# A gated graph, attention and memory layer on one core: the edge matrix counted in two copies, and the row products one slot later

## What is computed

```python
edge_index = jnp.stack([src, dst])
xn = _layernorm(x, axis=-1)
x = x + gnn(xn, edge_index, edge_type) + mix(xn)       # two gated graph layers; two blocks of linear attention and an MLP
x = x + memory(_layernorm(x, axis=-1))

# one graph layer; w[r] is a sum over 30 bases of 512 x 512, weighted by att
x_j = x[col]
msgs = [sigmoid(x_j @ gate_w[r])[:, None] * x_j @ w[r] for r in range(2)]
msg = jnp.where((edge_type == 0)[:, None], msgs[0], msgs[1])
agg = jax.ops.segment_sum(msg, row, num_segments=1250)
return agg + x @ root + bias

# memory: 8 heads, each picks 8 of 65536 pairs of keys; 64 rows for each node
inner = jnp.einsum('bd,bhkd->bhk', x, w_down[indices])
vals = jax.nn.relu(inner) * jax.nn.softmax(scores, axis=-1)
out = jnp.einsum('bhk,bhkd->bd', vals, w_up[indices])
```

## Time and profile before

| what | value |
|---|---|
| median of 3 runs | 3177.79 us |
| lowest and highest run | 3175.93 and 3196.16 us |
| the profiled execution, its own time | 3188.18 us |
| its span, first to last instruction | 3186.4 us |
| busy: PE, DVE, ACT, POOL | 2657.5, 1516.1, 700.5, 1010.8 us |
| mean granted TensorE clock | 0.926 |

### The profile page before, as it was taken

The page is one execution under the profiler, slowest core; times in us unless marked ns, Lnnn a source line. Parts: engine busy times, 40 slices in busy tenths (PEclk is TensorE's granted clock), DMA queues, the critical chain, the costliest instruction groups (busy, mean ns, idle before and its releaser), DMA issues.

```text
span 3186.4 us, 28032 instructions
## 1 busy us (share of the span) xinstructions
PE 2657.5 (83%) x8756; PEld 1463.4 (46%) x8756; DVE 1516.1 (48%) x3729; ACT 700.5 (22%) x1527; POOL 1010.8 (32%) x823
## 2 busy tenths in 40 slices
PE   2897887998770299999899888789898998998887
PEld 1564555665330044444366455554544544454322
DVE  3556448999200000000122545157657656666675
ACT  0233222121210000110033422123232323322322
POOL 0003343444344200000000000026566556656676
PEclk9898998999895599999999989899999999999999
DMA  9601306676210123023300040038898898889998
GB/s 209 204 0 21 89 1 190 200 216 187 43 7 1 32 78 79 0 62 112 92 1 0 0 148 0 7 110 314 284 329 312 297 314 308 309 311 332 344 366 349
DMA packets 237785, 498.58 MB, mean 156 GB/s; under 512 B 98553, under 2 KB 98928, under 8 KB 233546
## 3 DMA queue, kind: packets, MB, share of 16 engines
q0 software_dynamic: 158720, 336.03, 31.5%
q1 hardware_dynamic: 76425, 156.38, 16.5%
q10 hardware_dynamic: 2550, 5.12, 0.4%
HBM read 476.77 MB, written 20.34 MB: 156 GB/s over the span
## 4 chain that ended last, share of the span: by engine, by line
PE 49%; DMA 26%; DVE 11%; issue 7%; POOL 3%; ACT 2%; another core or an unknown queue 1%; SPq 1%; POOLq 0%; DVEq 0%; ACTq 0%
DMA adj<-e_cnt,e_idx 21%; PE bank L1018 10%; PE bank L1243 10%; PE bank L1233 3%; PE bank L1223 3%; PE bank L1003 2%; PE bank L581 2%; PE bank L1180 2%; PE bank L562 2%; PE bank L550 2%; PE bank L557 2%; PE bank L1192 2%; DVE qv L1471 2%; DMA qv<-in_L_ffn_rows,qv 2%; PE bank L770 1%
## 5 line engine op out<-in xcount | busy, mean ns | idle before, releaser
L283 POOL DMA_INDIRECT adj<-e_cnt,e_idx x160 | 344.2, 2151 | 740.4 <-DMA adj<-e_cnt,e_idx 446.8
L1243 PE MATMUL bank<-qv,stage 125*125 125x512 f32 x640 | 346.2, 633 | 65.6 <-DVE qv L1479 31.2
L1318 ACT ACTIVATE stage<-ident,qv 125x125 f32<-125x125 f32 x640 | 242.4, 397 | 481.7 <-DVE qv L1471 253.6
L1018 PE MATMUL bank<-big,wreg 125*125 125x512 f32 x400 | 173.4, 596 | 159.2 <-DMA wreg<-adj 159.2
L1471 DVE SCALAR_TENSOR_TENSOR qv<-qv 125x512 f32<-125x512 f32 x320 | 237.2, 745 | 143.8 <-DMA qv<-in_L_ffn_rows,biasb 74.4
L1143 POOL MEMSET wreg<- 64x2048 f32 x2 | 3.6, 1800 | 916.2 <-DVE h L700 916.1
L852 DVE SCALAR_TENSOR_TENSOR qv<-wreg,att_b,qv 128x2048 f32<-128x2048 f32 x120 | 276.9, 2349 | 6.9 <-DVE qv L852 0.2
L1149 POOL DMA_INDIRECT qv<-in_L_ffn_rows,qv x160 | 164.8, 1030 | 218.8 <-DVE qv L1413 113.9
L1243 PEld LDWEIGHTS bank<-qv,stage 125*125 125x125 f32 x640 | 113.8, 195 | 208.1 <-ACT stage L1318 91.2
L1149 POOL DMA_INDIRECT qv<-in_L_ffn_rows,biasb x160 | 163.9, 1025 | 112.7 <-PE bank L1243 90.7
L1018 PEld LDWEIGHTS bank<-big,wreg 125*125 125x125 f32 x400 | 75.6, 189 | 257.0 <-issue 257.0
(11 more groups left out here) (220 smaller groups left out, 4232.2 us busy)
## 6 DMA issues: line engine op xcount, KB each, us to landing
wreg<-in_L_gnn_basis SPq DMA_DIRECT2D x60, 1024.0 KB, 5.6
big<-in_L_mix_W SPq DMA_DIRECT2D x4, 4096.0 KB
adj<-wreg SPq DMA_DIRECT2D x5, 2187.5 KB
wreg<-adj SPq DMA_DIRECT2D x10, 1093.8 KB
qv<-adj SPq DMA_DIRECT2D x10, 1093.8 KB
big<-cells_t SPq DMA_DIRECT2D x1, 8750.0 KB
adj<-e_cnt,e_idx POOLq DMA_INDIRECT x160, 3.7
qv<-in_L_ffn_rows,qv POOLq DMA_INDIRECT x160, 5.9
```

The costliest lines, as they stand in the source:

```text
L283: nc.gpsimd.indirect_dma_start(out=adj, out_offset=bass.IndirectOffsetOnAxis(ap=e_idx[:, g:g + 1], axis=0), in_=e_cnt[:, g:g + 1], in_offs ...
L1018: mm = nc.tensor.matmul(psum[j][0:P, :], slabs[gl][:, j, c, :], zrel[:, c, :], start=(c == 0), stop=(c == COLT - 1))
L1243: nc.tensor.matmul(psum[7][0:P, :], diags[:, s % DRING, :], ring[s % RING][0:P, DIM:ROW], start=(s == 0), stop=(s == SLOTS - 1), skip_grou ...
L1318: nc.scalar.activation(diags[:, s % DRING, :], ident[0:P, 0:P], ACT.Relu, scale=inner[:, s:s + 1]).then_inc(p_diag, 1)
```

## The change

There are three edits.

1. **Two copies of the matrix.** A second matrix `adj_b` is made and zeroed (ten more DMAs on SP). Group g is added to `adj` or `adj_b` by turns, and waits for group g - 2. At the end GpSimd waits for both copies and issues ten DMAs that add `adj_b` onto `adj`, 272 rows of 1250 floats each (the last 52). SP waits for these before the first slab.
2. **The cell numbers.** They are copied to 128 partitions by one DMA, not to 112 and 13 by two. The 32 merges of the first pair of tiles move behind its values and norm, between its eight maxima of the key products (L493 before); those of the other pairs stay.
3. **The memory's slots.** TensorE puts `row` of slot s behind the pieces of slot s + 1 (`LAG = 1`). The turn of the next tile moves from slot 1 to slot 0, the eight queries from slots 2 to 9 to slots 1 to 5, the search of scores starts at slot 13 and not 11, its tail at 38 and not 35, the exponentials at 45 and not 42, and the take at slot 1 and not 3.

```diff
@@ adjacency_pool
             pool.wait_ge(s_idx, 4)
-            pool.wait_ge(s_adjz, 5 * 32)
+            pool.wait_ge(s_adjz, 5 * 64)
             for g in range(GROUPS):
-                if g:
-                    pool.wait_ge(s_adj, g * 16)
+                if g >= 2:
+                    pool.wait_ge(s_adj[g % 2], g // 2 * 16)
                 nc.gpsimd.indirect_dma_start(
-                    out=adj, out_offset=bass.IndirectOffsetOnAxis(ap=e_idx[:, g:g + 1], axis=0), in_=e_cnt[:, g:g + 1],
-                    in_offset=None, bounds_check=CELLS + 127, oob_is_err=True, compute_op=ALU.add).then_inc(s_adj, 16)
+                    out=(adj, adj_b)[g % 2], out_offset=bass.IndirectOffsetOnAxis(ap=e_idx[:, g:g + 1], axis=0), in_=e_cnt[:, g:g + 1],
+                    in_offset=None, bounds_check=CELLS + 127, oob_is_err=True, compute_op=ALU.add).then_inc(s_adj[g % 2], 16)
+            for n in range(2):
+                pool.wait_ge(s_adj[n], GROUPS // 2 * 16)
+            for n in range(SUMS):
+                rows = slice(272 * n, min(272 * n + 272, CELLS // 1250))
+                nc.gpsimd.dma_start(adj_rows[rows, :], adj_b_rows[rows, :], accum_op=ALU.add, max_dma_last_dim=5000).then_inc(s_sum, 16)
@@ setup_sp
-            for rows, count in zip(ROWS, (112, P - 112)):
-                sp.dma_start(cellb[rows, :, 0:CHUNK * P],
-                             cells_t.rearrange("g p -> (g p)").partition_broadcast(count).rearrange("q (c w) -> q c w", c=PAIRS)).then_inc(s_cellb, 16)
+            sp.dma_start(cellb[:, :, 0:CHUNK * P], cells_t.rearrange("g p -> (g p)").partition_broadcast(128).rearrange("q (c w) -> q c w", c=PAIRS)).then_inc(s_cellb, 16)
...
                 for rows, count in zip(ROWS, (112, P - 112)):
-                    sp.dma_start(adj_zero[n][rows, :, :], zbuf[rows, :].unsqueeze(1).to_broadcast([count, 4, CELLS // (20 * P)])).then_inc(s_adjz, 16)
+                    for zero in (adj_zero, adj_b_zero):
+                        sp.dma_start(zero[n][rows, :, :], zbuf[rows, :].unsqueeze(1).to_broadcast([count, 4, CELLS // (20 * P)])).then_inc(s_adjz, 16)
@@ attn1_dve
-                    if l == 0:
+                    if l == 0 and not first:
                         merge_dve(dve, i, c * CHUNK // KC, CHUNK // KC)
...
                 for n in range(8):
                     j, c = n // 4, n % 4
+                    if l == 0 and first and n < 7:
+                        merge_dve(dve, i, 4 * n + 4 * (n > 0), 4 + 4 * (n == 0))
@@ gcn_sp
-                sp.wait_ge(s_adj, 16 * GROUPS)
+                sp.wait_ge(s_sum, 16 * SUMS)
@@ mem
-        TURN_AT = 1
-        QUERY_AT = [2 + hh for hh in range(PKH)]
+        LAG = 1
+        TURN_AT = 0
+        QUERY_AT = [1 + hh - hh // 2 for hh in range(PKH)]
         SCORE_AT = [10 + 3 * hh for hh in range(PKH)]
-        TAIL_AT = 35
-        EXP_AT = 42
+        SEARCH_AT = SCORE_AT[0] + 3
+        TAIL_AT = SEARCH_AT + 25
+        EXP_AT = TAIL_AT + 7
...
-        TAKE_AT = 3
+        TAKE_AT = 1
@@ mem_pe
-                    row(t, s)
+                    late(t * SLOTS + s - LAG)
```

More of the change, by code:

```diff
@@ L208, in build @@
         s_adjz = sem("adjacency_zeroed")
-        s_adj = sem("group_added")
+        s_adj = [sem(f"group_added_{n}") for n in range(2)]
+        s_sum = sem("copies_added")
         s_ln = sem("ln0_step")
@@ L215, in build @@
         ROWS = (slice(0, 112), slice(112, P))
-        cellb = big[0:P, :].rearrange("p (c w) -> p c w", c=PAIRS)
+        cellb = big[:, :].rearrange("p (c w) -> p c w", c=PAIRS)
         CHUNK = GROUPS // PAIRS
@@ L472, in norm1, with pair @@
                                             rs[:, 0, ds(i * 2 + j, 1)], ALU.subtract, ALU.mult).then_inc(m["z"], 1)
-            def pair(i, last):
+            def pair(i, first, last):
                 for c in range(KC):
@@ L496, in attn1_dve @@
             norm1(0)
-            with dve.Fori(0, PAIRS - 1) as i:
-                pair(i, False)
-            pair(PAIRS - 1, True)
+            pair(0, True, False)
+            with dve.Fori(1, PAIRS - 1) as i:
+                pair(i, False, False)
+            pair(PAIRS - 1, False, True)
             dve.wait_ge(m["kmx"], l * ADDS["kmx"] + 4 * TILES)
@@ L1244, in row, with late @@
                                  skip_group_check=True).then_inc(p_up, 1)
+            def late(n):
+                if n >= 0:
+                    row(n // SLOTS, n % SLOTS)
             for _ in half(0):
@@ L1260, in mem_pe @@
                 for s in range(SLOTS):
-                    for _ in range((s == TURN_AT) + (s in QUERY_AT) + (s in SCORE_AT)):
+                    for _ in range((s == TURN_AT) + QUERY_AT.count(s) + SCORE_AT.count(s)):
                         next(ahead, None)
@@ L1269, in mem_pe @@
                     pass
+            for n in range(LAG):
+                late(TILES * SLOTS - LAG + n)
         def mem_act(act):
```

11 lines of the change are left out of this document (7 added, 4 removed).

## The result

| | before | after |
|---|---|---|
| median of the runs beside each other | 3185.72 us (4 runs, 3175.93 to 3196.16) | 3045.79 us (4 runs, 3042.31 to 3047.5) |
| ratio, 95% interval | | 0.9549 [0.9519, 0.958] |
| profiled execution, own time | 3188.2 us | 3042.31 us |
| its span | 3186.4 us | 3040.5 us |

The changed kernel is 4.5% faster: 140 us, where 161 were forecast. 3045.79 lies in the range, on the slow side of the forecast. As a ratio it is 0.955; the forecast was 0.949, and the rivals with crowded bases (3042) and with a memory that gains nothing (3044) stood at 0.957 and 0.958.

A forecast was written before the change was run, and what follows sets the result against it. Bound by a chain of group latencies before the slabs, VectorE in the bases, TensorE in the memory; 3188.2 - 10 - 159 + 35 - 27 = 3027, for the median 3017 us, range 2960 to 3090.

The forecast's parts named there:

- crowded bases: Rival: turns by packet let the sum crowd out the bases' loads beside it; 3042 us, chance 0.15.
- a memory that gains nothing: Rival: the memory's new slots gain nothing because its DMA engines are already at 0.89 to 0.95; 3044 us, chance 0.14.
- The gap, -159: Before the first slab product: TensorE's 159 us wait goes in full, as the sum ends before 900 us.
- The groups' pace, 2.47 then 2.8: Edge-matrix groups: about 95 at 2.47 us, then 65 at 2.8 beside the bases, the last landing near 672 us.
- the chain's 240 / 43 = 5.6 us: Groups beside the bases: the old chain's time per group, halved by two chains to 2.79 us.
- The sum itself, 82 us: Adding adj_b onto adj: 12.5 MB as two streams at 304 GB/s, 82 us of all DMA engines.
- The sum beside the bases, +35: Stretch of the bases: the sum delays their loads, on the path, by 35 us, bounds 0 and 73.
- the first rival: The sum crowds out the bases: 0.29 of the time left them, sum 115 us, 53 to 63 us short; chance 0.15.
- the 9 us of places already loaded: Stretch of the bases: about two bases already loaded in a ring, subtracted from the sum's delay.
- The set-up, -10: Start of the kernel: the first merges' later place lets pair 1 start 12 us earlier, taken as 10; the single DMA nothing.
- The memory, -27: Memory slots: 24.5 us from takes at tile crossings and 2 from waits for diagonals, 27 in all.
- The two chains do not overlap: Rival: groups still take 5.18 us each and the sum follows alone; 3223 us, chance 0.08 together with a slow adding DMA.

The follow-up runs named there:

- sum_spaced: The changed kernel with each adding DMA issued only when the one before it has landed, one in flight; 3007.48 us, 0.9416.
- no_sum: The changed kernel without the ten adding DMAs, slabs loaded from the first copy alone, so the odd groups are missing; 2996.97 us, 0.9361.
- same_again: The changed kernel run again with nothing edited, as a control; 3036.92 us, 0.949.
- sum_late: The changed kernel with the ten adding DMAs waiting until VectorE has added the last base; 3055.76 us, 0.9567.
- old_slots: The changed kernel with the third edit, the memory's slots, undone; 3057.61 us, 0.9546.
- rows_1000: The changed kernel with the sum's DMAs split in rows of 1000 bytes instead of 5000 by max_dma_last_dim; 3002.65 us, 0.9417.
- spaced_turn: sum_spaced with the memory's turn of the next tile one slot later (1 instead of 0); 3019.09 us, 0.9446.
- old_merge: The changed kernel with the first pair's merges back between the key copies, cell numbers still copied by one DMA; 3041.38 us, 0.9521.
- two_copies: The changed kernel with the cell numbers copied by two DMAs to 112 and 13 partitions again; 3042.94 us, 0.9489.

## Why the prediction was right, and where it was not

The changed kernel's own ratio is 0.949 to 0.955; the forecast was 3017 / 3177.8 = 0.949. The main step, the gap, was right for its reason. That the rest comes so near is partly luck: by the account above the memory gave 25 us less than forecast and the sum cost 6 more, while the set-up gave 5.5 more and block 1's clock 10, which was no part of the forecast. Step by step:

- **The gap, -159: right.** It is measured as 159.5, and the reason holds: groups and sum were done at 822 us, 143 before the first slab product.
- **The groups' pace, 2.47 then 2.8: too fast.** It is 2.3 us from 350 to 450, but 3.3 ahead of that (250 to 350, with one stretch of 13.6 and one of 7.9) and 3.5 from 540 to 740, 3.08 over all. The 95th group, due at 488, started at 514.5; that is 27 of the 73 us by which the sum came late. The other part arose beside the bases, and there the step that failed is the chain's 240 / 43 = 5.6 us for a landing beside the bases: with two chains it is 2 x 3.5 = 7.0, and GpSimd waited 32.0 + 18.3 + 2.4 = 52.7 us for landings in those 200. This cost nothing, since only the end of the sum mattered; the sum fell at 745 and not at 672, still among the bases.
- **The sum itself, 82 us: near, by two errors that cancel.** 745.4 to 822 are 77, 12.5 MB at 162 GB/s of bytes stored; but the 82 were meant for a sum that has the engines alone. From 748 to 750 us of sum_spaced it does, and stores 0.41 MB (81 packets) in 2 us, 205 GB/s: an estimate of 61 us for all of it. That is about half of the bases' 396 GB/s, so the factor of two streams fits, and the 304 GB/s to which it was applied were too low. The bases' turns in between stretch the 61 to 77.
- **The sum beside the bases, +35: mis-sized, and by the wrong rule.** Measured 41.4, 40 by no_sum. The forecast let the two share time evenly, and put turns by packet in the first rival because "the size of a turn is not seen". The counts show that packets go one to one. That rival was the right mechanism, and its 53 to 63 us were too much. It gave the bases 0.29 of the engines' time; that is their share of the bytes (0.30), while of the time they have 0.213 / (0.836 + 0.213) = 0.20. And it took the sum to be stretched to 115 us, but it lasts 77 us whether its neighbour has 71 GB/s (same_again) or 24 (sum_late, 1.81 MB in 77 us). At an equal count, packets take 0.836 x 320 / 708 = 0.38 us of an engine and 0.213 x 320 / 707 = 0.10, so the bases' turns lengthen the sum by a quarter at most. Short by 77 x (1 - 71 / 209) = 51 us, less the 9 us of places already loaded, gives 42. (209 GB/s is the mean from 660 to 740 us in no_sum.)
- **The set-up, -10: mis-sized, for a wrong cause.** 15.5 us were gained here, and 18 in same_again (pair 4 at 204.2). The step that failed is "one DMA to 128 partitions instead of two to 125 moves 2.4% more; I take nothing for it". It lands 27 us after its issue, and that alone brings pair 1 from 116.5 to 95.0. The merges' new place would have been worth 15 us without it and is worth nothing with it; the forecast's 10 us stood on the place alone.
- **The memory, -27: too much.** 17 us in tiles 1 to 6 are as the crossings were reckoned; the rest was put on tiles where the rows' loads end last, and does not show there. Over twelve traces with the new slots the memory takes 1041 to 1055 us, mean 1048, against 1054.0 and 1062.7 with the old ones. Over all, 21 us between same_again and old_slots, 1.5 between the two first traces, whose last three tiles differed by 15 us the other way. The rival "the memory gains nothing" is right for the last third alone.
- **The rivals on the other side.** "The two chains do not overlap" fell with the pace of 2.3 us.

**Something better than both.** sum_spaced (0.9416) and rows_1000 (0.9417) lie below the changed kernel (0.949 to 0.955) and come within 0.006 of no_sum (0.936), in which there is no sum; their traces show why. Both together were not tried.

## What to carry to other kernels

When a big transfer is put beside loads that the path needs, count packets and not bytes: in every stretch counted here in which both queues had work they got one packet each, so the transfer with the bigger packets took the time, and the queue of small packets suffered most. Two remedies cost a line or two each: keep a single DMA of the bulk in flight, or cut its rows below those of its neighbour. Both make the bulk itself slower, and worked here because it had time to spare. And a stretch in which the engines look idle is no cover if a few short loads in it are what TensorE waits for next.

## What was not expected of the hardware

- The step from one to two adding DMAs in flight changes the waits for bases from 0 (3.9 in spaced_turn) to 43 us; two or ten are the same.
- One DMA to 128 partitions (10 MB) lands after 27 us, at twice the rate of the two it replaces, with the DMA engines full in both cases; the merges wait 1.15 us and not 26.01 (old_merge); with two DMAs to 112 and 13 partitions VectorE waits 5.9 us for them even at the later place (two_copies).
- Rows of 250 numbers that lie one behind the other are joined to packets of 5000 bytes: the number of rows in the access pattern does not set the packet.
- In rows_1000, GpSimd issued five DMAs of 1360 rows in 7.67 us and then stood 62.66 us before the sixth, with no wait in the program; with 272 rows each the ten went out in 9.4 us. What it stood for the profile does not name.

```profile
730.19 7.67 POOL L294 DMA_DIRECT2D adj<-adj_b  x5 [2.37 <-DMA adj_b<-e_cnt,e_idx]
800.52 6.99 POOL L294 DMA_DIRECT2D adj<-adj_b  x5 [62.66 <-issue]
```
